# A transformer block and a convolution block on one core: where a loop on TensorE turns, ones in one lane instead of sixteen, and two weight loads sent later

## The chip, the core and the metric

The kernel runs on one core of one Trainium2 chip. A core has five engines with their own instruction queues: TensorE (PE, with its weight loads shown as PEld), VectorE (DVE), ScalarE (ACT), GpSimd (POOL) and SyncE (SP), which here only sends DMAs. They meet through semaphores. The metric is the device time of one execution in microseconds, the median of several runs.

## The reference

The input x is (4, 48, 128, 128) in float32. Two blocks follow each other.

```python
# block 1: windows of 8x8 tokens, 4 heads of 12 channels, 48 channels
h = layernorm(xf); q, k, v = split(h @ qkv_w.T + qkv_b)
attn = softmax(q * hd**-0.5 @ k.T + bias)
xf = xf + (attn @ v) @ proj_w.T + proj_b
m = gelu(layernorm(xf) @ fc1_w.T + fc1_b)     # 48 -> 192
xf = xf + m @ fc2_w.T + fc2_b                 # 192 -> 48
# block 2: 48 -> 288 -> 48 channels, batch norms folded into scale and shift
h = relu(bn1(w1 . x)); h = relu(bnd(depthwise3x3(h))); return x + bn2(w2 . h)
```

## The kernel before

**Three stages.** Attention takes the first 780 us of the profile, the MLP the time to 1133 us, the convolution block the rest. Attention and the other two stages are separate blocks with a barrier between them. The MLP and the convolution share one block: each engine runs its MLP program and then its convolution program, except that Pool, which has no work in the MLP, runs the convolution's preparations meanwhile.

**Attention** works on 128 groups of 8 windows (512 tokens). Each engine has one function `step(i, s)`, which handles several groups at once in different states: on PE (L336), in this order, the scores of group i (L343), a transpose of the outputs of group i - 2 (L349) and of the normalized input of group i + 2 (L356), the transposes of the probabilities of group i - 1 (L332), the output projection (L369), queries and keys of group i + 2 (L379), the weighted values of group i - 1 (L391) and the values of group i + 1 (L398). The scores are eight products, each of 64 columns of weights and 256 columns moved; float32 products appear as two matmul records each. VectorE reads the scores twice (L430 takes their maximum, L437 subtracts it); PE's next scores wait for the latter through `sub_done`. `schedule` (L215) writes out the steps -4 to 5, runs a loop over the groups 6 to 121 with two steps per turn, and writes out the rest. So PE branches back every second step, just ahead of the scores. Before the step given as `at` (0 for PE, -1 for VectorE and ScalarE) an engine runs `begin`: VectorE and ScalarE copy the bias table into the key tiles (L244, L507), and PE waits for these four copies (`bias_put`).

**The MLP** works on 64 strips of 8 image rows (two groups each). SyncE sends for the tokens of strip j + 3 (L608, 448 KB) into one of two buffers as soon as the transposes of strip j + 1 are through (`turned`); PE's step has the transposes (L644), the second product (L655) and the first product (L670) of different strips. The sum of a strip is ready when VectorE (L710) raises `mlp_done`, which inside the stage is called `y_done`; SyncE then stores it as image rows (L619). The loop has four strips per turn.

**Pool meanwhile** (L934 on) sets constants, sends 25 small loads (L953), the last of which fills the lanes 96 to 111 of `h1` with ones from DRAM (768 KB), sends two of the three tiles of depthwise matrices (`mats`, L955, 896 KB each), clears y, and waits for the stored first image (L963). The 25 loads are waited for near the MLP's end (`roots_on_act`).

**The convolution** cuts the image into patches of 10 x 10 pixels, so that a channel's patch is a column of 100 lanes (PIN). The depthwise filter of a channel is one product at L1127: `mats` (taps placed in a matrix of 112 rows and 64 columns, row 100 of which holds the shift) times `h1` (100 lanes of pixels; lane 100 must hold ones). The rows 101 to 111 of `mats` are zero. There are 288 such products per half image, 4608 records in all.

Of the kernel before, what the change touches and what calls it, by code (L numbers as in the profile page):

```python
# [39 lines left out]
PAIRS = GW // (2 * WS)  # L40
# [9 lines left out]
PIN, POUT = (PH + 2) * (PW + 2), PH * PW  # L50
PC, PR = 8, 16
PATCHES = PC * PR
MROWS = 112
HALF = PC * PW
SC = HALF + 2
CH = 96
CHUNKS = HID1 // CH
TCH = 32
LOADS = CH // TCH
# [7 lines left out]
def wait(eng, sem, n):  # L67

    if not isinstance(n, int) or n >= 1:
        eng.wait_ge(sem, n)  # L70
# [60 lines left out]
def attention(nc, d):  # L131

    with ExitStack() as ctx:
# [41 lines left out]
        bias_put = sem("bias_put")  # L175
        stored = [sem(f"mid_stored{s}") for s in range(2)]
        keys_put = [sem(f"keys_put{s}") for s in range(2)]
# [24 lines left out]
        def keys_of(i, s):  # L202

            return 16 * NH // 2 * (i - s) + 16 * NH
# [10 lines left out]
        def schedule(eng, step, begin=None, at=0):  # L215

            for i in range(-4, 6):
                if begin and i == at:
                    begin(eng)
                step(i, i % 2)  # L220
            with eng.Fori(6, GROUPS - 7, 2) as i:
                step(i, 0)
                step(i + 1, 1)
            for i in range(GROUPS - 6, GROUPS + 3):
                step(i, i % 2)
# [94 lines left out]
        @block.tensor  # L320
        def _(pe):
            pe.wait_ge(w_ready, 6)
            pe.wait_ge(rows_loaded, 16 * 4)
            pe.wait_ge(ident_put, 1)
            pe.wait_ge(fixed, FIXED)

            def turn_probs(i, s, k):

                for p in range(PAIRS // 2 * k, PAIRS // 2 * (k + 1)):
                    for h in range(2):  # L330
                        at = 256 * (p % 2) + P * h
                        mm = nc.tensor.transpose(ps_p[:, k, at:at + P], prob[1 - s][:, NH * p + 2 * h:NH * p + 2 * h + 2, :],  # L332
                                                 ident[:, :])
                mm.then_inc(pT_ready, 1)

            def step(i, s):  # L336
                if has(i):
                    pe.wait_ge(q_copied, i + 1)
                    pe.wait_ge(keys_put[s], keys_of(i, s))
                    wait(pe, sub_done, i)  # L340
                    for n in range(2 * PAIRS):
                        p, w = divmod(n, 2)
                        mm = nc.tensor.matmul(ps_s[NT * w:NT * w + NT, p // 2, 256 * (p % 2):256 * (p % 2) + 256],  # L343
                                              qa[s][:, NT * n:NT * n + NT], kb[s][:, n, :, :], start=True, stop=True)
                    mm.then_inc(s_ready, 1)
                if has(i - 2):
                    pe.wait_ge(on_done, i - 1)
                    for a in range(PAIRS // 2):
                        mm = nc.tensor.transpose(ps_oT[:, P * a:P * a + P], on[:, 2 * a:2 * a + 2, :], ident[:, :])  # L349
                    mm.then_inc(oT_ready, 1)  # L350
                if has(i + 2):
                    pe.wait_ge(xn_done, i + 3)
                    if has(i):
                        pe.wait_ge(v_copied, i + 1)
                    for a in range(PAIRS // 2):
                        mm = nc.tensor.transpose(ps_xT[:, P * a:P * a + P], xn[s][:, 2 * a:2 * a + 2, :], ident[:, :])  # L356
                    mm.then_inc(xnT_ready, 1)
                if has(i - 1):
                    pe.wait_ge(exp_done, i)
                    wait(pe, pT_copied, 2 * i - 2)  # L360
                    turn_probs(i, s, 0)
                if has(i - 1):
                    turn_probs(i, s, 1)
                if has(i - 2):
                    pe.wait_ge(oT_copied, i - 1)
                    if has(i + 2):
                        pe.wait_ge(xnT_copied, i + 3)
                    for a in range(PAIRS // 2):
                        mm = nc.tensor.matmul(ps_y[:, 2 * C * a:2 * C * a + 2 * C], oT[:, P * a:P * a + P], w_o[:, :],  # L369
                                              start=True, stop=True)  # L370
                    mm.then_inc(y_ready, 1)
                if has(i + 2):
                    pe.wait_ge(xnT_copied, i + 3)
                    wait(pe, q_copied, i + 2)
                    wait(pe, k_copied, i + 2)
                    for a in range(PAIRS // 2):
                        for e in range(2):
                            r = slice(ONE * e, ONE * e + ONE)
                            mm = nc.tensor.matmul(ps_k[0:112, e, P * a:P * a + P], w_qk[r, :], xnT[s][r, P * a:P * a + P],  # L379
                                                  start=True, stop=True)  # L380
                    mm.then_inc(qk_ready, 1)
                elif has(i):
                    pe.wait_ge(v_copied, i + 1)
                if has(i - 1):
                    pe.wait_ge(pT_copied, 2 * i)
                    pe.wait_ge(v_copied, i)
                    for p in range(PAIRS):
                        for h in range(2):
                            for w in range(2):
                                at = 2 * VE * (2 * p + h)  # L390
                                mm = nc.tensor.matmul(ps_o[NT * w:NT * w + NT, at:at + 2 * VE], probT[:, p, h, NT * w:NT * w + NT],  # L391
                                                      vb[1 - s][:, p, h, w, :], start=True, stop=True)
                    mm.then_inc(o_ready, 1)
                if has(i + 1):
                    wait(pe, res_done, i - 1)
                    for a in range(PAIRS // 2):
                        for w in range(2):
                            mm = nc.tensor.matmul(ps_v[NT * w:NT * w + NT, 2 * C * a:2 * C * a + 2 * C],  # L398
                                                  xnT[1 - s][:, P * a + NT * w:P * a + NT * w + NT], w_v[:, :],
                                                  start=True, stop=True)  # L400
                    mm.then_inc(v_ready, 1)

            schedule(pe, step, lambda pe: pe.wait_ge(bias_put, 4))

        @block.vector
        def _(dve):
# [338 lines left out]
def conv(nc, d):  # L745


    with ExitStack() as ctx:
# [6 lines left out]
        q = {n: sb(f"q_{n}", [CH, C]) for n in "gvt"}  # L755
# [11 lines left out]
        h1 = sb("h1", [P, CH, PATCHES])  # L767
# [167 lines left out]
        def _(pool):  # L935
# [11 lines left out]
            loads += [(q[n][:, :], d[f"bn2_{n}"].partition_broadcast(CH)) for n in "gv"]  # L947
            loads += [(c2[n][r:r + C, :], d[f"bn2_{n}"].rearrange("(c a) -> c a", a=1)) for n in "gbmv" for r in (0, ONE)]
            loads += [(dn[n], d[f"{n}d"].partition_broadcast(MROWS)) for n in "vgmb"]
            loads += [(h1[CH:MROWS, :, :].rearrange("q c n -> q (c n)"), d["ones"].partition_broadcast(MROWS - CH))]  # L950
            assert len(loads) == 25
            for dst, src in loads:
                pool.dma_start(dst, src).then_inc(w_loaded, 16)  # L953
            for s in range(LOADS - 1):
                pool.dma_start(mats[s][0:MROWS, :, :], d["taps"][s]).then_inc(mats_begun[s], 16)  # L955
            nc.gpsimd.memset(y[:, 0:H // 2, :], 0.0).then_inc(y_stored[0], 32)
            pool.wait_ge(y_stored[0], 32)
            nc.gpsimd.memset(y[:, H // 2:H - PH, :], 0.0).then_inc(y_done, 1)
            pool.wait_ge(y_done, 1)
            nc.gpsimd.memset(y[:, H - PH:H, :], 0.0).then_inc(y_stored[1], 32)  # L960
            pool.wait_ge(y_stored[1], 32)
            for s in range(2):
                pool.wait_ge(img_stored[s], 32 * (H // WS // 2))  # L963
            for j in range(PR):
# [118 lines left out]
        def _(pe):  # L1083
# [29 lines left out]
            def depthwise(k, d):  # L1113

                if d % (DEPTHS // LOADS) == 0:
                    pe.wait_ge(mats_scaled, LOADS * k + d // (DEPTHS // LOADS) + 1)
                if d == 0:
                    emptied(k, 0)
                if d >= 2:
                    emptied(k, d - 1)  # L1120
                for n in range(DUNIT // 2):
                    if d == 1 and n == 4:
                        pe.wait_ge(y_done, NSTEP * k + 1)
                    for u in range(2):
                        ch = DUNIT * d + DUNIT // 2 * u + n
                        bank = psum[POUT * u:POUT * u + POUT, 4 * (d % 2) + u + 2 * (n // 4), :]
                        mm = nc.tensor.matmul(bank[:, n % 4:4 * PATCHES:4], mats[ch // TCH][0:MROWS, ch % TCH, :],  # L1127
                                              h1[0:MROWS, ch, :],
                                              start=True, stop=True)
                        if (n + 1) % (DUNIT // 2 // PARTS[d]) == 0:  # L1130
                            mm.then_inc(unit_ready, 1)
# [199 lines left out]
```

## Time and profile before

| | us |
|---|---|
| median of 3 runs | 2026.35 |
| lowest and highest | 2024.22, 2032.85 |
| the profiled execution | 2029.93 |
| its span (first to last instruction) | 2028.0 |
| granted clock of TensorE over it | 0.987 |

| engine | busy us | share of the span |
|---|---|---|
| PE | 1925.4 | 95% |
| PEld | 1602.3 | 79% |
| DVE | 1445.8 | 71% |
| ACT | 1363.7 | 67% |
| POOL | 647.0 | 32% |

The profile is that of one execution. A page gives sums over the whole span; the views behind it give single stretches. PE's digits in the page's 40 slices are 9 nearly everywhere, except for the very start and for the slices 16 and 17, where the MLP begins. Busy times of PE are modelled, so that a PE that is always busy can still run later or earlier; the starts of its instructions tell more.

### The profile page before, as it was taken

How to read it: one execution, taken by the hardware profiler on the slowest of the kernel's cores; microseconds unless marked ns; L12 is line 12 of the kernel's file. 1: busy time of each engine (PE TensorE's matmuls, PEld its weight loads, DVE VectorE, ACT ScalarE, POOL GpSimd, SP SyncE). 2: the span in 40 equal slices, each digit the busy share in tenths (PEclk: the TensorE clock that was granted, in tenths of full speed). 3: DMA queues.
4: the chain of work that ended last, by engine and by line, in shares of the span. 5: the costliest groups of instructions: out<-in, count | busy, mean ns of one | idle time of the engine just before them, and what ended most of it. 6: DMA issues, size and time to landing. Idle time of an engine off the chain costs nothing.

```text
span 2028.0 us, 76431 instructions
## 1 busy us (share of the span) xinstructions
PE 1925.4 (95%) x29704; PEld 1602.3 (79%) x29704; DVE 1445.8 (71%) x2586; ACT 1363.7 (67%) x2838; POOL 647.0 (32%) x869
## 2 busy tenths in 40 slices
PE   5999999999999996799999899999999999999998
PEld 4888888888888884455555799898989899999987
DVE  5999999999999995455556665555656556566554
ACT  2777778777777884466666666666666566666665
POOL 4333333333333336013000342533424333425230
PEclk9999999999999997899999999999999999999999
DMA  2222222222222225656555344535455445455431
GB/s 65 68 75 74 75 75 75 75 72 74 75 75 75 75 71 117 145 138 162 139 133 131 91 91 108 124 87 128 98 109 132 101 102 128 96 128 106 105 100 33
DMA packets 286441, 199.46 MB, mean 98 GB/s; under 512 B 225991, under 2 KB 275672, under 8 KB 276488
## 3 DMA queue, kind: packets, MB, share of 16 engines
q1 hardware_dynamic: 282114, 189.12, 37.0%
q0 software_dynamic: 2368, 6.98, 1.6%
q8 instruction: 154, 2.52, 0.5%
q10 hardware_dynamic: 1750, 0.39, 0.1%
q14 instruction: 55, 0.45, 0.1%
HBM read 129.10 MB, written 54.72 MB: 91 GB/s over the span
## 4 chain that ended last, share of the span: by engine, by line
PE 56%; ACT 2%; DMA 1%; DVE 1%; issue 1%; SPq 0%; ACTq 0%; DVEq 0%
PE psum L1108 14%; PE psum L1127 13%; PE psum L1153 9%; PE psum L670 6%; PE psum L655 5%; PE psum L1162 5%; PE psum L644 3%; ACT h2T L1209 1%; DMA room<-tok_mid 1%; DVE h L877 1%; DMA room<-in_ident 0%; ACT room L736 0%; DVE room L877 0%; ACT room L740 0%; DVE room L702 0%
## 5 line engine op out<-in xcount | busy, mean ns | idle before, releaser
L926 POOL TENSOR_TENSOR mats<-mats,dscale 112x2048 f32<-112x2048 f32 x72 | 260.8, 3622 | 350.1 <-DMA mats<-in_taps 347.7
L1108 PE MATMUL psum<-ew,xp 64*100 64x96 f32 x6144 | 322.3, 253 | 15.4 <-DVE h L877 11.1
L1209 ACT ACTIVATE h2T<-psum 96x1024 f32<-96x1024 f32 x192 | 195.6, 1019 | 188.4 <-PE psum L1162 188.4
L877 DVE TENSOR_SCALAR h<-psum 100x384 f32<-100x384 f32 x384 | 211.8, 557 | 149.6 <-PE psum L1108 140.3
L1108 PEld LDWEIGHTS psum<-ew,xp 64*100 64x100 f32 x6144 | 295.1, 165 | 25.1 <-DVE h L877 14.1
L1127 PE MATMUL psum<-h,mats 112*64 112x128 f32 x4608 | 269.5, 276 | 6.5 <-issue 4.9
L1127 PEld LDWEIGHTS psum<-h,mats 112*64 112x64 f32 x4608 | 253.9, 138 | 15.4 <-issue 6.2
L876 ACT ACTIVATE room<-psum 64x512 f32<-64x512 f32 (+1 forms) x384 | 206.0, 537 | 85.1 <-PE psum L1127 78.7
L343 PE MATMUL psum<-kb,qa 128*64 128x256 f32 x2048 | 253.1, 383 | 1.3 <-DVE prob L437 0.8
L877 DVE TENSOR_SCALAR room<-psum 64x512 f32<-64x512 f32 (+1 forms) x288 | 174.2, 605 | 71.8 <-PE psum L1127 65.8
L876 ACT ACTIVATE h<-psum 100x384 f32<-100x384 f32 x384 | 186.6, 486 | 45.8 <-PE psum L1108 33.3
L1153 PE MATMUL psum<-h2T,pw 128*64 128x128 f32 x3072 | 197.3, 277 | 17.8 <-ACT h2T L1209 9.4
L343 PEld LDWEIGHTS psum<-kb,qa 128*64 128x64 f32 x2048 | 154.2, 137 | 50.4 <-issue 2.7
L1153 PEld LDWEIGHTS psum<-h2T,pw 128*64 128x64 f32 x3072 | 168.6, 137 | 30.1 <-ACT h2T L1209 13.7
L520 POOL TENSOR_TENSOR xn<-cen,rstd 128x192 f32<-128x192 f32 x128 | 64.9, 507 | 349.1 <-ACT rstd L493 349.1
L430 DVE TENSOR_REDUCE top<-psum 128x16 f32<-128x1024 f32 x128 | 156.7, 1224 | 12.4 <-PE psum L343 9.3
L736 ACT ACTIVATE room<-psum,room 128x512 f32<-128x512 f32 x128 | 81.0, 685 | 115.4 <-PE psum L670 115.3
L437 DVE TENSOR_TENSOR prob<-psum,top 128x1024 f32<-128x1024 f32 x128 | 155.8, 1217 | 0.1
L465 ACT ACTIVATE probT<-psum 128x512 f32<-128x512 f32 x256 | 151.2, 601 | 0.0
L699 DVE COPY room<-psum 48x512 f32<-48x512 f32 x64 | 44.6, 697 | 141.1 <-PE psum L644 141.1
L391 PE MATMUL psum<-vb,probT 128*64 128x26 f32 x4096 | 143.4, 219 | 1.6 <-issue 1.0
L391 PEld LDWEIGHTS psum<-vb,probT 128*64 128x64 f32 x4096 | 129.9, 138 | 18.6 <-issue 1.2
(152 smaller groups left out, 3334.8 us busy)
## 6 DMA issues: line engine op xcount, KB each, us to landing
mats<-in_taps SPq DMA_DIRECT2D x69, 896.0 KB, 6.3
tok_mid<-mid SPq DMA_DIRECT2D x128, 224.0 KB, 1.9
room<-tok_mid SPq DMA_DIRECT2D x64, 448.0 KB, 3.7
piece<-img_mid SPq DMA_DIRECT2D x196, 63.8 KB, 2.3
img_mid<-room SPq DMA_DIRECT2D x128, 97.5 KB, 2.7
kb<-kk SPq DMA_DIRECT2D x512, 24.0 KB
out<-yc SPq DMA_DIRECT2D x32, 384.0 KB, 4.4
scratch<-in_x_tokens SPq DMA_DIRECT2D x126, 96.0 KB, 1.9
```

What stands on the lines that cost most here:

```text
L343: mm = nc.tensor.matmul(ps_s[NT * w:NT * w + NT, p // 2, 256 * (p % 2):256 * (p % 2) + 256], qa[s][:, NT * n:NT * n + NT], kb[s][:, n, :, ...
L391: mm = nc.tensor.matmul(ps_o[NT * w:NT * w + NT, at:at + 2 * VE], probT[:, p, h, NT * w:NT * w + NT], vb[1 - s][:, p, h, w, :], start=True ...
L430: nc.vector.tensor_reduce(top[s][:, :], sc, AX_X, ALU.max).then_inc(top_done, 1)
L437: nc.vector.tensor_tensor(prob[s][:, :, :], sc, bc(top[s][:, :], 2, NT), ALU.subtract)\
L465: nc.scalar.activation(probT[:, 2 * k:2 * k + 2, :, :].rearrange("q p h n -> q (p h n)"), ps_p[:, k, :], ACT.Copy)\
L876: return nc.scalar.activation(dst, src, ACT.Relu)
L877: return nc.vector.tensor_scalar(dst, src, 0.0, None, ALU.max)
L926: nc.gpsimd.tensor_tensor(m, m, bc(scale[0:MROWS, at:at + TCH], 2, POUT), ALU.mult).then_inc(mats_scaled, 1)
L1108: mm = nc.tensor.matmul(ring[(j + u) % 4][0:PIN, p:4 * CH:4], xp[hx][rows, 2 * j + p, :], w1[rows, c, :], start=True, stop=True)
L1127: mm = nc.tensor.matmul(bank[:, n % 4:4 * PATCHES:4], mats[ch // TCH][0:MROWS, ch % TCH, :], h1[0:MROWS, ch, :], start=True, stop=True)
L1153: mm = nc.tensor.matmul(ps_y[n % 2][64 * r:64 * r + 64, at:at + PCOLS], w2[:, c, :], h2T[n % 2][:, r, at:at + PCOLS], start=True, stop=True)
L1209: nc.scalar.activation(h2T[n % 2][0:CH, :, :], turned_at(n, last)[0:CH, :, 0:POUT * PART], ACT.Copy).then_inc(copied, 1)
```

## The change

Three edits:

- On PE, the function with the scores is split in two halves of four products. `step(i)` begins with the second half of group i and ends with the first half of group i + 1, together with that half's waits. The order of PE's instructions stays, but the loop's edge now lies between the two halves. PE's wait for the bias stands before step -1 instead of step 0.
- The ones are loaded into lane 100 of `h1` alone, and the depthwise product contracts over 101 lanes instead of 112.
- Pool sends the first two loads of `mats` after it has cleared y, and waits for six and for twelve finished strips of the MLP before them.

```diff
-            def step(i, s):
+            def scores(i, s, part):
                 if has(i):
-                    pe.wait_ge(q_copied, i + 1)
-                    pe.wait_ge(keys_put[s], keys_of(i, s))
-                    wait(pe, sub_done, i)
-                    for n in range(2 * PAIRS):
+                    if part == 0:
+                        pe.wait_ge(q_copied, i + 1)
+                        pe.wait_ge(keys_put[s], keys_of(i, s))
+                        wait(pe, sub_done, i)
+                    for n in range(PAIRS * part, PAIRS * part + PAIRS):
                         p, w = divmod(n, 2)
                         mm = nc.tensor.matmul(ps_s[NT * w:NT * w + NT, p // 2, 256 * (p % 2):256 * (p % 2) + 256],
                                               qa[s][:, NT * n:NT * n + NT], kb[s][:, n, :, :], start=True, stop=True)
-                    mm.then_inc(s_ready, 1)
+                    if part:
+                        mm.then_inc(s_ready, 1)
+
+            def step(i, s):
+                scores(i, s, 1)
                 if has(i - 2):
...
                     mm.then_inc(v_ready, 1)
-
-            schedule(pe, step, lambda pe: pe.wait_ge(bias_put, 4))
+                scores(i + 1, 1 - s, 0)
+
+            schedule(pe, step, lambda pe: pe.wait_ge(bias_put, 4), -1)
...
-            loads += [(h1[CH:MROWS, :, :].rearrange("q c n -> q (c n)"), d["ones"].partition_broadcast(MROWS - CH))]
+            loads += [(h1[PIN:PIN + 1, :, :].rearrange("q c n -> q (c n)"), d["ones"])]
...
-            for s in range(LOADS - 1):
-                pool.dma_start(mats[s][0:MROWS, :, :], d["taps"][s]).then_inc(mats_begun[s], 16)
             nc.gpsimd.memset(y[:, 0:H // 2, :], 0.0).then_inc(y_stored[0], 32)
...
             pool.wait_ge(y_stored[1], 32)
+            for s in range(LOADS - 1):
+                pool.wait_ge(mlp_done, 6 * (s + 1))
+                pool.dma_start(mats[s][0:MROWS, :, :], d["taps"][s]).then_inc(mats_begun[s], 16)
...
-                        mm = nc.tensor.matmul(bank[:, n % 4:4 * PATCHES:4], mats[ch // TCH][0:MROWS, ch % TCH, :],
-                                              h1[0:MROWS, ch, :],
+                        mm = nc.tensor.matmul(bank[:, n % 4:4 * PATCHES:4], mats[ch // TCH][0:PIN + 1, ch % TCH, :],
+                                              h1[0:PIN + 1, ch, :],
...
-        "ones": np.ones(CH * PATCHES, np.float32),
+        "ones": np.ones((1, CH * PATCHES), np.float32),
```

## Rows read from the trace of the kernel before

**Rows 1.** The page: busy time, share of the span, instructions.

```profile
PE 1925.4 (95%) x29704; PEld 1602.3 (79%) x29704; DVE 1445.8 (71%) x2586; ACT 1363.7 (67%) x2838; POOL 647.0 (32%) x869
```

**Rows 2.** Windows: busy us (count) per engine, granted clock, DMA share, GB/s.

```profile
110.00:730.00 620.00, 620.00 (x8657) 513.52 (x8655) 599.56 (x1191) 494.10 (x1301) 209.77 (x433) 1.00 0.24 74
```

**Rows 3.** Timeline, PE's weight loads: start us, us, what, [idle before, releaser].

```profile
412.50 0.20 PEld L349 LDWEIGHTS psum<-ident,on 128*128 128x128 f32 x2 [0.38 <-issue]
...
418.40 0.20 PEld L349 LDWEIGHTS psum<-ident,on 128*128 128x128 f32 x2 [0.39 <-issue]
...
424.04 0.20 PEld L349 LDWEIGHTS psum<-ident,on 128*128 128x128 f32 x2 [0.38 <-issue]
...
429.77 0.20 PEld L349 LDWEIGHTS psum<-ident,on 128*128 128x128 f32 x2 [0.39 <-DVE on L417]
...
435.42 0.20 PEld L349 LDWEIGHTS psum<-ident,on 128*128 128x128 f32 x2 [0.39 <-issue]
```

**Rows 4.** Timeline, start of the MLP: Pool's matrix loads and PE's transposes.

```profile
806.18 1.05 POOL L955 DMA_DIRECT2D mats<-in_taps  x2
...
809.52 1.08 PE L644 MATMUL psum<-room 128*112 128x128 f32 x8
...
827.10 1.93 PE L644 MATMUL psum<-room 128*112 128x128 f32 x8 [12.54 <-DMA room<-tok_mid]
...
839.92 1.08 PE L644 MATMUL psum<-room 128*112 128x128 f32 x8
```

**Rows 5.** DMAs from 765 to 900 us: queue, count, KB each, median us to landing.

```profile
mats<-in_taps POOLq DMA_DIRECT2D x2, 896.0 KB, 18.6
...
h<-in_ones POOLq DMA_DIRECT2D x1, 768.0 KB, 13.3
```

**Rows 6.** The chain of waits that ended last: start us, us, what.

```profile
805.96 20.91 DMA room<-tok_mid
...
1667.14 8.92 PE psum L1127 x160
```

**Rows 7.** Windows, the stall in the MLP (columns as in rows 2).

```profile
809.50:827.10 17.60, 5.06 (x38) 2.80 (x37) 2.89 (x4) 4.72 (x8) 1.55 (x2) 0.79 0.96 197
```

**Rows 8.** Timeline, PE's transposes of two strips with the MLP loop's edge between.

```profile
864.77 1.08 PE L644 MATMUL psum<-room 128*112 128x128 f32 x8
...
869.74 1.08 PE L644 MATMUL psum<-room 128*112 128x128 f32 x8
```

**Rows 9.** Timeline, attention: scores on PE and VectorE's first reading of them.

```profile
445.13 1.90 PE L343 MATMUL psum<-kb,qa 128*64 128x256 f32 x16
...
447.07 1.23 DVE L430 TENSOR_REDUCE top<-psum 128x16 f32<-128x1024 f32 x1
...
450.81 1.95 PE L343 MATMUL psum<-kb,qa 128*64 128x256 f32 x16
...
452.79 1.22 DVE L430 TENSOR_REDUCE top<-psum 128x16 f32<-128x1024 f32 x1
```

**Rows 10.** Timeline, start of attention around the copies of the bias.

```profile
32.23 0.69 PE L356 MATMUL psum<-ident,xn 128*128 128x128 f32 x2
...
32.96 1.93 ACT L507 ACTIVATE kb<-psum 64x1024 f32<-64x1024 f32 x2
33.06 2.35 DVE L244 COPY kb<-psum 64x1024 f32<-64x1024 f32 x2
...
37.93 3.60 PE L343 MATMUL psum<-kb,qa 128*64 128x256 f32 x16 [0.55 <-DMA kb<-kk]
```

**Rows 11.** Groups by line and form: busy us, mean ns, idle before.

```profile
L1127 PEld LDWEIGHTS psum<-h,mats 112*64 112x64 f32 x4608 | 253.9, 138 | 15.4 <-issue 6.2 <-DVE yc L1246 1.3 <-DVE yc L1251 1.3
...
L343 PEld LDWEIGHTS psum<-kb,qa 128*64 128x64 f32 x2048 | 154.2, 137 | 50.4 <-issue 2.7
```

**Rows 12.** The line L608, strip loads from 835 to 1100 us (54 of them).

```profile
DMA to landing us min/median/max: 3.3/3.7/4.6
```

**Rows 13.** DMAs from 1140 to 1990 us (columns as in rows 5).

```profile
mats<-in_taps SPq DMA_DIRECT2D x69, 896.0 KB, 6.3
```

## The prediction, made before the change was run

> **What bounds the kernel now.** I first read the head of the page: TensorE is busy for 95% of the span [rows 1]. An edit can therefore pay only where it shortens PE's own stream or removes one of the few places where PE stands still. The view of the windows confirms this for attention: between 110 and 730 us PE is busy for all 620.00 us, VectorE for 599.56 [rows 2]. "Busy" is modelled there, so I looked at start times instead. In the timeline of PE's weight loads the transpose at L349 comes once per step; from one to the next the starts are 5.90, 5.64, 5.73 and 5.65 us apart [rows 3]. The loop makes two steps per turn, and the long intervals (5.90, 5.73) hold the loop's edge, where PE branches back ahead of the scores. A step with no edge takes 5.645 us, so the edges cost 0.25 and 0.08 us in turn.
>
> Next I looked in the MLP, where the page's digits for PE fall. There PE waits 12.54 us for a strip of tokens [rows 4]. The chain of waits names the load: sent at 805.96, landed 20.91 us later [rows 6]. Pool's load of ones goes out just before it, its two loads of depthwise matrices at 806.18 [rows 4]; the ones take 13.3 us to land, the matrices 18.6 (median of two) [rows 5]. Over the window of the stall the DMA engines are 96% busy [rows 7].
>
> **The change, part by part.**
>
> **1. The loop's edge on PE.** No matmul is added or removed and their order stays; only the edge moves, from ahead of the eight score products (16 matmul records, 1.90 us [rows 9]) to behind the first four. In rows 3 four steps with two edges take 435.42 - 412.50 = 22.92 us; four without would take 4 x 5.645 = 22.58. That is 0.34 us for two edges, 0.17 each. The loop turns 58 times and branches back 57 times: 57 x 0.17 = 9.6 us. Will it be covered in its new place? Today the matmuls queued in front of the edge are the value products at L398, short ones with 96 columns; the new place has half of the scores in front, some 0.95 us of work with 256 columns, and no wait right behind it. The nearest row is the MLP's loop, whose edge lies behind matmuls of 256 columns (L670) too: from strip to strip the transposes start 4.97 us apart, and at an edge (between 864.77 and 869.74) no more [rows 8]. So I take the whole 9.6 us. The bounds are 0, if the edge costs the same anywhere, and 9.6.
>
> What is late next? VectorE. It has an edge of its own at the same step: from L430 to L430 it takes 452.79 - 447.07 = 5.72 us there [rows 9]. If that and the 5.65 of the other step were VectorE's own pace, two steps would need 11.37 us instead of PE's 11.29, and the gain would be 57 x (11.46 - 11.37) = 5.1 us instead of 9.6. But both starts of L430 lie 0.03 to 0.04 us behind the end of PE's scores (445.13 + 1.90 = 447.03; 450.81 + 1.95 = 452.76) [rows 9]: VectorE still waits for PE in both steps, and its own pace is quicker. I take 9.6 and leave 5.1 as a case.
>
> The waits ahead of the first half of the scores (queries, keys, the previous subtraction) stand at the same place in the stream, and nothing new is queued behind them.
>
> **2. The wait for the bias, one step earlier.** PE now waits for the copies of the bias table (L244, L507) before it transposes the second group's input. Those transposes start at 32.23, the copies end at 33.06 + 2.35 = 35.41 [rows 10]. The transposes slip by 3.2 us. ScalarE, however, reads them only after its own bias copies (32.96 + 1.93 = 34.89) and so slips just from 34.9 to about 35.45 + 0.69 = 36.1, 1.2 us. The first scores stand at 37.93 because their keys landed only then (a wait of 0.55 us for the DMA) [rows 10], which takes some of the slip up. The cost is about 1.0 us, once; bounds 0 and 3.2.
>
> **3. Ones in one lane.** The load of ones shrinks from 768 KB in 16 lanes to 48 KB in one. The depthwise product contracts over 101 lanes instead of 112. A weight load of 64 columns takes 138 ns with 112 lanes and 137 with 128 [rows 11], so lanes don't show, and I cost this at nothing; bounds plus and minus 2 us.
>
> **4. The two matrix loads, later.** Pool no longer sends 2 x 896 KB at 806.18. With these and the ones gone, the strip sent at 805.96 stands behind Pool's small parameter loads only. An undisturbed strip load lands in 3.7 us (3.3 to 4.6) [rows 12]. It is sent for as soon as the transposes that empty its buffer are through and is needed two strips later: 2 x 4.97 - 1.08 = 8.86 us of room. So the stall goes. It costs more than the 12.54 us seen: the transposes start at 809.52, 827.10 and, two strips on, 839.92, that is 30.40 us for three strips that take 3 x 4.97 = 14.91 elsewhere [rows 4, 8]. The difference is 15.5 us; it includes work at a lower clock after the stall (the transposes at 827.10 take 1.93 us, those at 839.92 1.08; the clock granted over the stall's window is 0.79 of 2.4 GHz) [rows 4, 7]. Some of the old congestion may stay, since parameter loads go out until just before: bounds 13.5 and 15.5, and I take 15.5.
>
> The loads return at the sixth and the twelfth strip, near 828 and 858 us. Each moves 896 KB against a strip's 448. Pool's queue holds nothing else there: behind the new waits comes only the wait for the first stored image, sixteen strips in, so nothing is late. What stands in danger is the strip load under way. In the old stall that load landed after 20.91 us, past the large ones, so I assume the worst order: the strip last. At the 197 GB/s of the stall's window [rows 7] 896 KB (0.92 MB) take 4.7 us; with the strip's own 3.7 that is 8.4 us, under the room of 8.86. A load of the same matrices in the last stage lands in 6.3 us beside other traffic [rows 13]. I take 0.5 us for both; bounds 0 and 3 us each.
>
> The Trainium skill speaks to this point ("DMA: Bandwidth & Descriptors", section "Queues, rings and completion order"): each DMA engine goes round between the queue rows that have work, packet by packet. By that rule a strip load keeps its share beside a large load and the two late loads cost nothing. The old stall doesn't bear that out: there the strip got out only with the large loads.
>
> **The sum.** -9.6 (edges) + 1.0 (bias) + 0 (lanes) - 15.5 (stall) + 0.5 (late loads) = -23.6 us. The profiled execution took 2029.93 us, which gives 2006.3. It lies 3.6 us above the median of the runs shown (2026.35), and the prediction is for a median: 2026.35 - 23.6 = **2002.7 us**.
>
> **Rivals.**
> - *VectorE takes over in attention.* For it: 599.56 of 620.00 us busy, and 5.72 us in its step with an edge. Against it: it waits for PE at L430 in that step too. 2002.7 + 4.5 = 2007.2.
> - *The stall comes back in part at strips six and twelve.* Its margin (8.4 against 8.86) is thin, and the image stores share the engines. A stall of 2 us each, and the lower clock behind it (as now, where 12.5 seen became 15.5), make some 3 us each: 2002.7 + 6 - 0.5 = 2008.2.
> - *The edge isn't covered.* If the branch stops PE's queue whatever is in it, the 9.6 us stay: 2012.3. The MLP's loop speaks against it.
> - *The strip is late for the parameter loads before it,* not for the ones and the matrices. Then the stall stays: 2002.7 + 15.5 = 2018.2. The sizes speak against it (2.5 MB of 3 MB sent around then are the loads that go).
> - *Slower.* 101 lanes, no round number, cost the array or its operand reads more than 112. To be slower by more than can be told this must cost (23.6 + 10) / 4608 = 7.3 ns for each depthwise record, on a pace of 8.92 us / 160 = 56 ns [rows 6]; the time is then 2037 us. Nothing speaks for it but that no contraction over such a number stands in the trace.
>
> **How the numbers follow.** Chances: forecast 0.60, VectorE 0.11, part of the stall back 0.12, edge not covered 0.08, stall not cured 0.05, slower 0.04. The low end is the forecast with the runs' own spread (2024.22 is 2.1 below the median) and the bounds of bias and lanes: 1998.5. The high end takes in the uncovered edge: 2012.5. About 0.5% (10 us, so 2016.2) is what a measurement of this kernel can tell from no change. Faster by more than that are the first four cases, 0.91; same 0.05; slower 0.04.
>
> **What would show it.** In attention all steps on PE 5.65 us apart, also at the edge; if VectorE took over, pairs of 11.37 us and waits of PE for VectorE. In the MLP no wait of PE for tokens beyond a microsecond, transposes 4.97 us apart from the third strip on, the strip sent near 806 landed in under 8 us, and the granted clock full to the end of the stage. The MLP's first transposes come some 8.6 us earlier than now, its end about 24. The depthwise products still take 8.92 us per 160. Wrong would be above all: an interval of over 5.7 us at the edge, or a strip load that lands more than 8.9 us after it was sent near the sixth or twelfth strip.

## The result, and the profile after

The changed kernel takes 2005.61 us (median of 4 runs, 2000.87 to 2013.33) against 2026.94 us (4 runs, 2024.22 to 2032.85). The ratio on record is 0.9869 with a 95% interval of 0.9844 to 0.9895, 1.3% faster. It isn't the quotient of these two medians: that is 0.9895, at the slow edge of the interval. Its profiled execution took 2007.32 us with a span of 2005.3, which is 22.7 us less than the span before.

The head of the page of the changed kernel, with the busy times of the engines and the granted clock in tenths:

```profile
span 2005.3 us, 76491 instructions
...
PE 1913.1 (95%) x29704; PEld 1584.4 (79%) x29704; DVE 1441.9 (72%) x2586; ACT 1365.1 (68%) x2838; POOL 647.0 (32%) x869
...
PEclk9999999999999997999999999999999999999999
```

PE's share is 95% as in rows 1: the time went out of busy parts (12.3 us) and idle ones (10.4 us) alike. I read it stage by stage, from the starts of PE's instructions.

**Attention.** The timeline of the weight loads at L354 (L349 before), which answers to rows 3:

```profile
414.10 0.20 PEld L354 LDWEIGHTS psum<-ident,on 128*128 128x128 f32 x2 [0.39 <-DVE on L423]
...
419.74 0.20 PEld L354 LDWEIGHTS psum<-ident,on 128*128 128x128 f32 x2 [0.39 <-issue]
...
425.39 0.20 PEld L354 LDWEIGHTS psum<-ident,on 128*128 128x128 f32 x2 [0.39 <-DVE on L423]
...
431.04 0.20 PEld L354 LDWEIGHTS psum<-ident,on 128*128 128x128 f32 x2 [0.38 <-issue]
```

All steps are 5.65 us apart, with an edge or without. Over the whole stage no step takes longer than 5.647 us. Before, 58 took more than 5.65 us, 9.64 us more in all; 57 of them hold an edge, the other one lies in the written-out start and makes 0.2 us of it. From the first of these transposes to the last it is 713.8 us instead of 723.4.

**The MLP.** The timeline around the strip load that stalled (L614, L608 before), the transposes (L650, L644 before) and Pool's loads, which answers to rows 4:

```profile
795.60 1.08 PE L650 MATMUL psum<-room 128*112 128x128 f32 x8
...
796.71 0.40 SPq L614 DMA_DIRECT2D room<-tok_mid  x1
797.07 0.50 POOL L959 DMA_DIRECT2D h<-in_ones  x1
...
800.57 1.08 PE L650 MATMUL psum<-room 128*112 128x128 f32 x8
...
805.66 1.06 PE L650 MATMUL psum<-room 128*112 128x128 f32 x8
...
820.54 0.53 POOL L968 DMA_DIRECT2D mats<-in_taps  x1 [19.02 <-DVE room L716]
820.55 1.08 PE L650 MATMUL psum<-room 128*112 128x128 f32 x8
821.81 0.41 SPq L614 DMA_DIRECT2D room<-tok_mid  x1
...
825.52 1.08 PE L650 MATMUL psum<-room 128*112 128x128 f32 x8
...
830.49 1.08 PE L650 MATMUL psum<-room 128*112 128x128 f32 x8
```

The strip sent at 796.71 took 8.7 us to land (the line of the landings below), and the transposes for it start 5.09 us after those before: 0.12 us late, not 12.5. The first late load goes out at 820.54. The strip sent 1.3 us behind it takes 8.0 us, and PE's transposes stay 4.97 us apart. Landings of strip loads from 795 to 860 us, and the DMAs from 765 to 900 us (answering to rows 5 and 12):

```profile
DMA to landing us min/median/max: 3.7/4.0/8.7
```

```profile
mats<-in_taps POOLq DMA_DIRECT2D x2, 896.0 KB, 7.9
...
h<-in_ones POOLq DMA_DIRECT2D x1, 48.0 KB, 8.6
```

Between the first and the last transposes of the MLP lie 316.4 us instead of 331.4. The window of the old stall, moved up with the kernel, has PE busy for 17.54 of 17.60 us at a granted clock of 1.00, where rows 7 have 5.06 at 0.79 (same columns):

```profile
799.60:817.20 17.60, 17.54 (x130) 9.79 (x128) 9.24 (x14) 11.84 (x19) 1.79 (x2) 1.00 0.71 170
```

**The last stage.** The depthwise products over 101 lanes cost what those over 112 did: 276 ns for a product's record in both traces, 138 ns for a weight load (rows 11). Groups by line and form:

```profile
L1134 PE MATMUL psum<-h,mats 101*64 101x128 f32 x4608 | 269.4, 276 | 6.8 <-issue 5.2 <-DVE room L883 0.8 <-DVE h L883 0.7
L1134 PEld LDWEIGHTS psum<-h,mats 101*64 101x64 f32 x4608 | 253.9, 138 | 15.5 <-issue 6.5 <-DVE yc L1258 1.3 <-DVE yc L1253 1.3
```

The balance of the two profiled executions, from the starts of PE's first and last instructions of each part:

| part | before | after | difference |
|---|---|---|---|
| start to the first transposes of `on` | 51.77 | 52.72 | +0.95 |
| to the last of them | 723.41 | 713.83 | -9.58 |
| to the MLP's first transposes | 13.64 | 12.96 | -0.68 |
| to the MLP's last transposes | 331.41 | 316.38 | -15.03 |
| to the first expansion | 13.56 | 13.57 | 0.0 |
| to the end | 894.18 | 895.89 | +1.7 |

### The profile page after: what moved, and what is told of

Its sections match the earlier page's. It is cut to its first block, busy times and chain, and to the rows that moved or that the text cites. A ratio compares the mean times of both kernels' runs of the same rounds, so it can differ in the third digit from the quotient of the medians.

```text
span 2005.3 us, 76491 instructions
## 1 busy us (share of the span) xinstructions
PE 1913.1 (95%) x29704; PEld 1584.4 (79%) x29704; DVE 1441.9 (72%) x2586; ACT 1365.1 (68%) x2838; POOL 647.0 (32%) x869
## 4 chain that ended last, share of the span: by engine, by line
PE 57%; ACT 2%; issue 1%; DVE 1%; DMA 0%; SPq 0%; ACTq 0%; DVEq 0%
PE psum L1115 14%; PE psum L1134 13%; PE psum L1160 9%; PE psum L676 6%; PE psum L661 6%; PE psum L1169 5%; PE psum L650 3%; ACT h2T L1216 1%; DVE h L883 1%; DMA room<-in_ident 0%; ACT room L742 0%; DVE room L883 0%; ACT room L746 0%; ACT h L882 0%; DVE room L708 0%
## 5 line engine op out<-in xcount | busy, mean ns | idle before, releaser
L1115 PE MATMUL psum<-ew,xp 64*100 64x96 f32 x6144 | 322.6, 253 | 15.5 <-DVE h L883 11.1
L1134 PE MATMUL psum<-h,mats 101*64 101x128 f32 x4608 | 269.4, 276 | 6.8 <-issue 5.2
L1134 PEld LDWEIGHTS psum<-h,mats 101*64 101x64 f32 x4608 | 253.9, 138 | 15.5 <-issue 6.5
L344 PE MATMUL psum<-kb,qa 128*64 128x256 f32 x2048 | 244.6, 381 | 0.6 <-DVE prob L443 0.6
L344 PEld LDWEIGHTS psum<-kb,qa 128*64 128x64 f32 x2048 | 140.8, 138 | 56.2 <-issue 1.9
L906 POOL COPY xp<-piece 128x400 f32<-128x400 f32 x128 | 67.6, 528 | 226.0 <-DMA piece<-img_mid 223.6
```

Source lines behind the costliest of these rows:

```text
L1115: mm = nc.tensor.matmul(ring[(j + u) % 4][0:PIN, p:4 * CH:4], xp[hx][rows, 2 * j + p, :], w1[rows, c, :], start=True, stop=True)
```

## Experiments

Each is told by its edit, against the kernel before or the changed kernel. A time is compared with that of the kernel before on the same chip. Where a run was executed once, its time alone says little, and I go by the stages of its profile. For the MLP I give the time from its first to its last transposes (331.4 before, 316.4 changed), for attention that between the first and last transposes of `on` (723.4 and 713.8).

**The parts alone.** First the new edge alone, that is the changed kernel with the ones in 16 lanes, the contraction over 112 lanes and the early matrix loads put back (in part):

```diff
-            loads += [(h1[PIN:PIN + 1, :, :].rearrange("q c n -> q (c n)"), d["ones"])]
+            loads += [(h1[CH:MROWS, :, :].rearrange("q c n -> q (c n)"), d["ones"].partition_broadcast(MROWS - CH))]
...
+            for s in range(LOADS - 1):
+                pool.dma_start(mats[s][0:MROWS, :, :], d["taps"][s]).then_inc(mats_begun[s], 16)
             nc.gpsimd.memset(y[:, 0:H // 2, :], 0.0).then_inc(y_stored[0], 32)
```

> Only the first edit of the change: PE's loop turns between the halves of the scores, the rest as before. Theory (the queued scores cover the edge; the two gains don't depend on each other): all steps of attention 5.65 us apart, 57 x 0.17 = 9.6 us less in the loop, 1.0 us more at its start, the stall in the MLP unchanged with some 12.5 us of waiting and 15.5 us of lateness; in all about -8.6 us (2018). Rival (the edge's gain is real only together with the loads, for instance since part of it is drift between executions): the loop's span shrinks by less than 7 us or the stall changes too.

Measured: 2022.72 us (10 runs) against 2030.99 (14 runs) of the kernel before, ratio 0.9948 (0.9928 to 0.9968), or -10.6 us. Attention takes 713.8 us. The stall stays: PE waits twice for tokens, 13.0 us in all, and the MLP takes 332.8 us.

Then the loads alone, with attention as before:

> Only the second and the third edit: ones in one lane (contraction over 101 lanes) and the two matrix loads at the sixth and twelfth strip; PE's loop turns ahead of the scores as before. Theory: the edge keeps costing 0.08 and 0.25 us in turn, the stall is gone, MLP from its first to its last transposes about 316 us instead of 331; in all about -15 us (2012). Rival: below 10 us gained, because the MLP's congestion is moved instead of removed.

Measured: 2015.24 us (4 runs), ratio 0.9921 (0.9890 to 0.9951), or -16.0 us. Attention 723.6 us, MLP 316.4 us, no wait for tokens. The two parts add up: 10.6 + 16.0 = 26.6 us on this chip by the ratios, and 0.0131 x 2027 = 26.6 us by the whole change's own ratio. Medians give less, 8.3 + 15.7 = 24.0 against 21.3; with intervals of 4 to 6 us either way on each ratio, neither sum is at odds with the whole. Each gain sits in its own stage.

**What makes an edge cost.** Two other places for the edge, both in the kernel before: between the halves of the weighted values, with short products in front and no wait behind; and behind all eight score products, with long ones in front and waits behind. The edit of the first, in part:

```diff
             def step(i, s):
+                weighted(i - 1, 1 - s, 1)
+                values(i - 1, 1 - s)
...
-                    for p in range(PAIRS):
...
+                weighted(i, s, 0)
```

> The kernel before, but PE's loop turns between the two halves of the weighted values (16 matmul records of 26 columns in front of the edge, no wait behind it). Theory (what is queued in front of the edge covers it, so long matmuls are needed): the short records cover at most 0.5 us, so the edge costs as much as before or more, 0.1 to 0.4 us per turn, 6 to 20 us over the loop. Rival (what costs is the waits and registers right behind the branch): no cost, all steps 5.65 us apart.

> The kernel before, but PE's loop turns behind all eight score products, ahead of the transposes that wait for on and xn. Theory (queued work covers the edge): 16 records of 256 columns stand in front, all steps 5.65 us apart, although waits stand right behind the edge. Rival (waits behind the branch cost): 0.1 to 0.3 us per turn remain.

Measured: both cost next to nothing. The timelines of the weight loads of `on`, first with the edge among the weighted values, then behind all scores:

```profile
413.43 0.20 PEld L377 LDWEIGHTS psum<-ident,on 128*128 128x128 f32 x2 [0.38 <-DVE on L430]
...
419.07 0.20 PEld L377 LDWEIGHTS psum<-ident,on 128*128 128x128 f32 x2 [0.39 <-issue]
...
424.73 0.20 PEld L377 LDWEIGHTS psum<-ident,on 128*128 128x128 f32 x2 [0.38 <-DVE on L430]
```

```profile
414.08 0.20 PEld L351 LDWEIGHTS psum<-ident,on 128*128 128x128 f32 x2 [0.39 <-DVE on L420]
...
419.73 0.20 PEld L351 LDWEIGHTS psum<-ident,on 128*128 128x128 f32 x2 [0.39 <-issue]
...
425.38 0.20 PEld L351 LDWEIGHTS psum<-ident,on 128*128 128x128 f32 x2 [0.39 <-DVE on L420]
```

The steps with an edge take 5.654 us in the first (0.008 more) and 5.646 in the second; attention takes 715.4 us (1.1 of the excess over 713.8 is its last step) and 714.3. The single executions took 2027.12 and 2018.83 us beside one of the kernel before with 2031.47; the first has a last stage of 901.5 us in its profile, which hides its gain in attention. So long products in front aren't needed, against my expectation for the first. The second falsifies the rival that waits behind an edge are enough to make it cost. Neither theory alone fits both. What is left is their sum, which the next run tries: the old place, but with the three waits ahead of the edge.

```diff
+            def scores_free(i, s):
+                if has(i):
+                    pe.wait_ge(q_copied, i + 1)
+                    pe.wait_ge(keys_put[s], keys_of(i, s))
+                    wait(pe, sub_done, i)
...
+                scores_free(i + 1, 1 - s)
```

> The kernel before, PE's edge at its old place (behind the value products, ahead of the scores), but the three waits of the scores stand ahead of the edge instead of behind it. Theory (the sequencer's whole time between two products counts, branch 0.36 us and waits 0.25 us together, against the 0.5 us of products queued in front): the same cost as before, 0.08 and 0.25 us in turn, some 9 us over the loop, or a little less. Rival (only what stands behind the branch counts): all steps 5.65 us apart, 713.8 us from the first to the last transposes of on.

```profile
411.02 0.20 PEld L352 LDWEIGHTS psum<-ident,on 128*128 128x128 f32 x2 [0.39 <-issue]
...
416.76 0.20 PEld L352 LDWEIGHTS psum<-ident,on 128*128 128x128 f32 x2 [0.39 <-DVE on L421]
...
422.40 0.20 PEld L352 LDWEIGHTS psum<-ident,on 128*128 128x128 f32 x2 [0.39 <-issue]
...
428.14 0.20 PEld L352 LDWEIGHTS psum<-ident,on 128*128 128x128 f32 x2 [0.38 <-DVE on L421]
```

Measured: 5.74 and 5.65 us in turn. Each edge costs 0.095 us from the third turn on (the first two more), 5.8 us over the loop; attention takes 719.6 us, and the single execution took 2020.81 us against 2031.80 (7 runs). With nothing behind the edge but products it still costs, so the rival falls. It costs less than before, where the edges took 9.4 us, and less than the theory of the sum gave (some 9 us), and the alternation of 0.08 and 0.25 is gone. So the place of the waits has a part.

The instruction records of single turns show where the time goes. Before, the first weight load of the scores starts 0.59 or 0.54 us after the branch began, in turn, while the last value product started at 0.515; here it starts at 0.33 with the last at 0.316, and the next load follows at 0.365. The first score product isn't even late here: it starts 0.360 us after the first value product, as in a step without an edge. Late is the second of the two records that each float32 product has. Without an edge the records start in pairs, at 0.360 and 0.368, 0.576 and 0.584, and so on to 1.871 and 1.879. Here they start at 0.360 and 0.464, 0.576 and 0.679, to 1.871 and 1.971: the pair that the edge pulled apart stays apart to the end of the scores, and that is the 0.09 us. Why it does, and why the old place cost 0.08 and 0.25 in turn, stays open. Among the weighted values the two loads behind the edge come at 0.34 and 0.36, nearly in their pace. There too the last product in front started 0.32 us after the branch began, so the time queued in front doesn't tell these two runs apart (0.008 and 0.095 us); what follows the edge does, products of 26 columns there and of 256 here. Behind half or all of the scores a microsecond or more of products is still queued when the branch begins.

**What made the strip late.** First both matrix loads at strip six, in the changed kernel:

```diff
-                pool.wait_ge(mlp_done, 6 * (s + 1))
+                pool.wait_ge(mlp_done, 6)
```

> The changed kernel, but both matrix loads go out at the sixth strip. Theory (a strip load lands only past the large bytes sent beside it, and has 8.86 us of room): 2 x 0.92 MB at 197 GB/s take 9.3 us, with the strip's own 3.7 it lands some 13 us after it is sent at the worst, about 11 if it is sent 1 to 2 us behind them; PE waits 2 to 4 us for tokens at one strip near 835 us, with a lower clock behind, 3 to 6 us lost. Rival (each queue gets its share of the engines packet by packet): the strip lands in some 8 us and PE does not wait.

Timeline, PE's wait in this run:

```profile
833.89 1.93 PE L650 MATMUL psum<-room 128*112 128x128 f32 x8 [3.69 <-DMA room<-tok_mid]
```

The strip landed after 12.4 us, and the MLP takes 321.1 us, 4.7 more; the time is 2010.11 us (3 runs), ratio 0.9898 (0.9868 to 0.9928). That is what the theory gave (11 to 13 us, 2 to 4 of wait, 3 to 6 lost), and it counts against a fair share for the strip load. The DMA records agree: in the first 5.5 us after the strip was sent, 143 of the matrices' packets (8192 bytes) began and three of the strip's (1792 bytes). Only in the next 4 us do they mix, 78 to 151. The room of 8.86 us is real, and one load at a time just fits in it: 8.0 us here, 7.5 to 8.5 over the profiles with late loads.

Then each of the old loads back at the start, by itself: the matrices early with the ones in one lane, and the ones in 16 lanes with the matrices late.

> The changed kernel, but the two matrix loads go out at the start of the MLP as before (the ones stay in one lane, 48 KB). Theory (the bytes of the large loads decide, whichever they are): 1.84 MB at 197 GB/s take 9.3 us, so the strip load sent at that time lands some 13 to 16 us later (small parameter loads are in flight too); PE waits 4 to 8 us at one strip instead of 12.5, and 7 to 11 us are lost. Rival (the load of ones made the stall, for its 16 lanes lie on few DMA engines): no wait of PE, as in the changed kernel.

> The changed kernel, but ones go into 16 lanes (768 KB) and the depthwise product contracts over 112 lanes, as before; the matrix loads stay late. Theory (bytes decide): 0.79 MB at 197 GB/s take 4 us more beside the parameter loads; the changed kernel's strip load of that moment took 8.7 us to land, so this one takes up to 12 us: PE waits 1 to 3 us at one strip. Rival (only the matrices matter): no wait. Rival (the ones made most of the stall): more than 6 us of wait. The depthwise products take the same 276 ns a record either way.

PE's waits, in this order:

```profile
813.62 1.57 PE L650 MATMUL psum<-room 128*112 128x128 f32 x8 [2.90 <-DMA room<-tok_mid]
```

```profile
809.62 1.92 PE L650 MATMUL psum<-room 128*112 128x128 f32 x8 [5.57 <-DMA room<-tok_mid]
```

Measured: with the matrices early PE waits 2.90 us and the MLP takes 320.4 us (4.0 more); with the ones in 16 lanes it waits 5.57 and takes 323.7 (7.3 more). Both lie outside what I expected, on opposite sides. The single executions took 2014.22 and 2014.76 us. The smaller transfer does the greater damage: 0.79 MB cost 5.57 us of waiting, 1.84 MB cost 2.90. Bytes at one rate, as in my sum, are not the measure. In the second run the ones needed 18.2 us to land:

```profile
h<-in_ones POOLq DMA_DIRECT2D x1, 768.0 KB, 18.2
```

The DMA records show how. The ones go as 16 packets of 49152 bytes, each 5.4 to 8.6 us long, while a matrix packet of 8192 bytes takes about 0.5 us. That suggested long packets as the cause, and so the same load in eight parts:

```diff
+            for n in range(8):
+                cols = slice(CH // 8 * n, CH // 8 * (n + 1))
+                loads += [(h1[CH:MROWS, cols, :].rearrange("q c n -> q (c n)"),
+                           d["ones"][CH // 8 * PATCHES * n:CH // 8 * PATCHES * (n + 1)].partition_broadcast(MROWS - CH))]
```

> The kernel with the ones in 16 lanes (768 KB, contraction over 112 lanes, late matrix loads), but the load of ones is cut into eight of 96 KB. In the whole form the trace holds 16 DMA packets of 49152 bytes, 5.4 to 8.6 us each, one per DMA engine. New theory (a strip load waits behind packets under way, and long packets are what held it): with packets of 6 KB the strip load of that moment lands in under 10 us instead of 14 to 16, and PE waits below 1 us instead of 5.6. Rival (the bytes, or the 16 lanes at one place of the memory, take the time): the ones still need 15 to 18 us and PE waits 4 to 6 us.

```profile
804.87 1.06 PE L650 MATMUL psum<-room 128*112 128x128 f32 x8 [0.80 <-DMA room<-tok_mid]
...
813.46 1.95 PE L650 MATMUL psum<-room 128*112 128x128 f32 x8 [3.58 <-DMA room<-tok_mid]
```

Measured: 4.4 us of waiting in two pieces, and the MLP takes 322.8 us instead of 323.7; the single execution took 2018.86 us. Of the two strip loads under way one came down from 14.2 to 9.5 us, the other only from 16.3 to 13.3, where I expected under 10. From the first send to the last landing the ones took 15.4 us instead of 18.2, which lies within the 13.3 to 18.8 of the uncut load in five other profiles. The new theory falls for the most part; the length of the packets is worth about a microsecond of waiting, if that. The packets are now 6144 bytes and take 0.77 us each, longer than the matrices' of 8192 bytes (0.58 here): the transfer itself is slow. Whether its destination in 16 neighbouring lanes or its source (the same 48 KB, read 16 times) makes it so wasn't tried and stays open. Its place in Pool's queue isn't enough: the load of 48 KB at the same place lands after 6.5 to 8.6 us.

**The wait for the bias** at its old point, ahead of the scores of group 0 instead of ahead of step -1:

> The changed kernel, but PE waits for the bias ahead of the first half of the scores of group 0 instead of ahead of step -1. Theory (the slip at the start comes from this wait alone): the transposes of the second group's input go back to about 32.3 us, the first transposes at the line of on start about 0.9 us earlier than in the changed kernel (51.8 instead of 52.7), everything behind them moves up by the same; about -1 us in all, below what the times can tell. Rival (the keys' DMA decides the first scores in any case): no difference at that transpose.

The timelines of the start, this run first, then the changed kernel (PE's transposes, the copies of the bias, the first scores):

```profile
32.62 0.69 PE L363 MATMUL psum<-ident,xn 128*128 128x128 f32 x2
...
33.45 2.35 DVE L244 COPY kb<-psum 64x1024 f32<-64x1024 f32 x2
...
38.28 3.68 PE L346 MATMUL psum<-kb,qa 128*64 128x256 f32 x16 [0.51 <-DMA kb<-kk]
```

```profile
33.45 2.35 DVE L244 COPY kb<-psum 64x1024 f32<-64x1024 f32 x2
...
35.86 0.69 PE L361 MATMUL psum<-ident,xn 128*128 128x128 f32 x2 [3.17 <-DVE kb L244]
...
38.84 2.77 PE L344 MATMUL psum<-kb,qa 128*64 128x256 f32 x12
```

The bias copies start at the same moment in both, so this is a clean pair: the transposes come 3.24 us later in the changed kernel, the first scores 0.56 us. The wait costs 0.5 to 0.6 us (52.72 against 52.20 at the first transposes of `on`), some half of what I expected; the rest of the 0.95 in the balance is a later start of the copies themselves (33.45 against 33.06 in rows 10). At the first scores the other profiles say the same: they start 5.38 to 5.39 us after the bias copies begin in all eight with the early wait, 4.79 to 4.87 in all five without. By the first transposes of `on` other delays lie on top: with the early wait these start anywhere from 51.67 to 52.72 us. The times can't tell it: 2007.26 us, ratio 0.9876 (0.9842 to 0.9910). Its first steps lost 0.4 us and its last one 1.1, and the run with the last stage written out has the same last step, so that isn't the wait's doing.

**A larger edge.** The last stage has a loop of three turns with thousands of instructions each. In the changed kernel I wrote it out on PE:

```diff
-            schedule(pe, first, chunk)
+            first()
+            for b in range(HALVES // 2):
+                for hx in range(2):
+                    for c in range(CHUNKS):
+                        chunk(b, hx, c, b == HALVES // 2 - 1 and hx == 1 and c == CHUNKS - 1)
```

> The changed kernel, with PE's loop of the last stage (three turns of some 222 us each, of thousands of instructions) written out. In the changed kernel PE stands still for 2.8 and 2.4 us where this loop turns back (237 and 459 us into the stage), with a lower clock behind, and for 1.7 to 3.1 us once per turn at a place without a branch. Theory (a branch far back costs a fetch of instructions that no queue covers): the two stands at the turns go, those between stay; 5 to 9 us less, near 1999. Rival (the stands are the fetch itself, wherever): nothing gained.

Timelines at the loop's first turn, the changed kernel and then this one:

```profile
1346.73 3.63 PE L1134 MATMUL psum<-h,mats 101*64 101x128 f32 x32 [2.76 <-issue]
```

```profile
1346.73 1.97 PE L1134 MATMUL psum<-h,mats 101*64 101x128 f32 x32 [0.75 <-issue]
```

Both long stands at the turns went (2.76 to 0.75, 2.41 to 0.73 us) and with them the lower clock behind: the granted clock over the 3.7 us from 1346.70 is 0.54 in the changed kernel and 1.00 here, and the same 32 records take 1.97 us instead of 3.63. The branch's own record at a turn of this loop takes 3.3 to 3.8 us in each of the twelve profiles that have the loop, 0.21 us in attention and in the MLP, and the stands there are 2.35 to 2.83 us in all twelve. That the far branch makes them is shown. The stands on "issue" without a branch didn't go: four of over half a microsecond with 9.9 us in all became seven with 11.3. The stage took 891.3 us instead of 895.9, but the twelve profiles with the loop have 890.6 to 902.1, so this difference isn't told from chance. The time is 2002.14 us (4 runs), ratio to the kernel before 0.9858 (0.9824 to 0.9891): beside the changed kernel's 0.9869 no gain can be told, and the 5 to 9 us that I expected aren't shown.

## Why the prediction was right

- **The sum.** Forecast -23.6 us for the profiled execution, -22.6 measured; -21.3 between the medians and -26.6 by the ratio (21.3 to 31.6 less); 2002.7 us against 2005.61, inside the range. That the profiled pair comes within 1 us is in part luck: the stall and the last stage each differ by several us from one profile to the next.
- **The edge** (forecast 9.6 us, though 57 x 0.17 is 9.7): 9.58 in the profile, of which 9.4 at the edges, and 713.8 us of attention again with the edge alone. The MLP's loop edge [rows 8] turned out to be the right row to go by. The reason I gave, long products in front, is sufficient (nothing is lost behind half or all of the scores) but not needed: short ones nearly do where no waits come on top. VectorE didn't take over: PE keeps 5.65 us in each step while VectorE is busy 604 of 620 us.
- **The bias** (forecast 1.0): 0.5 to 0.6. The term was mis-sized: the scores' wait for the keys' DMA, 0.51 us without the early wait, is gone with it, so it took up about half of the slip of some 1.1 us, more than I allowed.
- **The lanes** (forecast 0): 276 and 138 ns per record, nothing.
- **The stall** (forecast 15.5, with 0.5 for the late loads against it): 15.03 in the profile. The MLP takes 329.1 to 333.7 us in the five profiles with the old loads and 315.7 to 316.4 in the four with both load edits, so a pair could have shown anything from 12.7 to 18. The lateness behind the stall belonged to it, as said. The late loads cost nothing that shows at their strips. One sign that I named failed: the strip sent near 806 (796.71 here) landed after 8.7 us, not under 8, beside the parameter loads. It left 0.1 us, since the room is 8.86.
- **What was wrong in it** is the mechanism behind the margin: I put ones and matrices together as bytes at 197 GB/s. For the matrices that holds (8.0 us forecast as 8.4; 12.4 for two at once). The ones are a slow transfer of their own and made the larger part, 5.57 us against 2.90. Together they cost more (12.5, and 11.9 to 13.4 in the five profiles with both) than the sum of both (8.5); why isn't shown. Since the change removes both, the forecast didn't depend on the split.
- **Not in the sum:** +1.7 us in the last stage and -0.7 between the stages. PE's program of the last stage, the same but for the lanes, took from 890.6 to 902.1 us in the profiles of the twelve kernels that loop there, with stands of PE on "issue" in changing places. More of the difference between these profiles lies there than in any other stage with the same program, and I didn't settle what sets it.

## What to carry to other kernels

Where a saturated engine loops, compare the starts of one instruction per step: a turn that costs 0.1 to 0.2 us shows in no list of waits. Put the edge where a microsecond or more of products is queued in front (free here, waits behind it or not), or into the middle of a run of short equal products without waits (0.008 us here). Ahead of the long score products, with the same 0.32 us queued, it cost 0.095 us even without waits behind it. Before sending a large load beside a stream of small ones, compute the stream's room (here two strips less the transposes) and add the load's time at the rate that such a load has shown; send large ones one at a time where the room takes one. A fill of a few lanes from DRAM can cost more than a larger load over 112 lanes, as here, so fill only the lane that is needed.

## What the runs showed of the hardware

- PE's branch took 0.215 us by its record and about 0.33 us until the next product's weights began to load; with three waits behind it 0.54 or 0.59 us. Ahead of the scores 0.095 us of this was exposed without the waits and 0.08 or 0.25 with them; among short equal products it was 0.008, and behind a microsecond or more of queued products nothing.
- The same branch took 3.3 to 3.8 us by its record in a loop of thousands of instructions per turn, and PE stood for 2.35 to 2.83 us.
- A load of 768 KB into 16 lanes took 13.3 to 18.8 us where one of 48 KB into one lane, sent at the same place, took 6.5 to 8.6. One of 896 KB into 112 lanes, sent late and one at a time, took 7.1 to 8.8 us. Cut into packets of 6 KB the 768 KB took 15.4 us.
- The Trainium skill ("DMA: Bandwidth & Descriptors", section "Queues, rings and completion order") has the DMA engines go round between queues packet by packet. Beside one matrix load a strip load took 8.0 us. Beside two it took 12.4 us and PE waited 3.69, and hardly any of its packets began in the first 5.5 us, so the share didn't protect it here.
- The Trainium skill ("Runtime: NRT & Kernel Launch", section "Instruction fetch mechanics") says that a taken branch to a target outside the current window of instructions forces a fetch. The last stage's loop agrees: the branch records of 3.3 to 3.8 us and stands of 2.8 and 2.4 us at its turns, 0.75 without the branches. Attention's short loop shows nothing of that size. The records don't single out the fetch itself.
